# Adding the last six rounds' expert results into four sum rows per token, and reading the first ten rounds' rows early, in a fused attention and mixture-of-experts kernel

## The reference, cut to what matters

```
xe = jnp.zeros((E, CAP, H), x.dtype).at[sorted_e, pos].set(tok_sorted, mode='drop')
h = jax.nn.silu(jnp.einsum('ech,efh->ecf', xe, w1)) * jnp.einsum('ech,efh->ecf', xe, w3)
ye = jnp.einsum('ecf,ehf->ech', h, w2)
...
vals = jnp.where((pos < CAP)[:, None], vals, 0.0)
out = jax.ops.segment_sum(vals * flat_w[:, None], flat_t, num_segments=T)
shared = jax.nn.silu(x @ shared_gate.T) * (x @ shared_up.T) @ shared_down.T
return (out + shared).reshape(B, S, H)
...
x = x + _layernorm(_L0_ffn_ref(_layernorm(x, axis=-1), ...), axis=-1)
```

## Time and profile before

| what | us |
|---|---|
| median of three runs | 1123.37 |
| the profiled execution's own time | 1122.23 |
| its span, from first to last instruction | 1120.4 |
| first instruction of run_experts on TensorE | 948.8 |
| last DMA issue of run_experts on POOL ends | 1057.7 |
| first load of finish is issued | 1064.8 |
| last residual on VectorE ends | 1118.2 |

### The profile page before, as it was taken

How to read it: one execution, slowest core, us unless ns; L and a number is a source line. 1 busy time by engine, 2 the same in 40 slices (tenths; PEclk the granted TensorE clock), 3 DMA queues, 4 the chain that set the end, 5 groups by cost and what they waited for, 6 DMA issues and landing times. The chain is left out here.

```text
span 1120.4 us, 16485 instructions
## 1 busy us (share of the span) xinstructions
PE 911.1 (81%) x5190; PEld 289.5 (26%) x5190; DVE 816.9 (73%) x1314; ACT 685.9 (61%) x1416; POOL 555.9 (50%) x729
## 2 busy tenths in 40 slices
PE   5657999999999999999999999999986541745076
PEld 3311222222222222222222222222212321534043
DVE  6787888889889988988988998898841540322057
ACT  5714777777787777778778777777884210333113
POOL 6780020124356455645735554563576754456425
PEclk9867999999999999999999999999998665666578
DMA  5893432012332222222223212000222003410097
GB/s 140 262 250 63 118 80 62 15 38 47 83 110 87 90 90 55 59 49 82 82 91 104 49 39 50 5 6 14 79 82 91 2 3 90 119 51 13 17 400 275
DMA packets 107181, 96.35 MB, mean 86 GB/s; under 512 B 51406, under 2 KB 86512, under 8 KB 105046
## 3 DMA queue, kind: packets, MB, share of 16 engines
q1 hardware_dynamic: 89846, 88.12, 26.7%
q0 software_dynamic: 14336, 4.25, 1.8%
q10 hardware_dynamic: 2912, 2.93, 1.2%
HBM read 49.36 MB, written 65.24 MB: 102 GB/s over the span
## 5 line engine op out<-in xcount | busy, mean ns | idle before, releaser
L269 DVE TENSOR_REDUCE half_max<-s_pair 128x2 f32<-128x1024 f32 x512 | 602.0, 1218 | 77.8 <-PE s_pair L258 73.2
L1423 ACT ACTIVATE probs<-st_bank 128x512 f32<-128x512 f32 x1024 | 544.1, 602 | 170.3 <-PE st_bank L1519 157.2
L1285 POOL DMA_INDIRECT table<-rows,keys_i x256 | 255.5, 998 | 180.7 <-PE pv_bank L1528 67.5
L1519 PE MATMUL st_bank<-q_stack,k_stack 98*128 98x512 bf16 (+1 forms) x1024 | 324.0, 387 | 13.0 <-ACT probs L1423 4.9
L1528 PE MATMUL pv_bank<-probs,values 128*9 128x512 f32 x2048 | 267.7, 595 | 3.1 <-ACT unit_out L1358 2.8
L258 PE MATMUL s_pair<-k_stack,q_stack 64*128 64x512 bf16 x1024 | 202.5, 395 | 28.7 <-DVE half_max L269 26.4
L258 PEld LDWEIGHTS s_pair<-k_stack,q_stack 64*128 64x128 bf16 x1024 | 49.2, 93 | 344.3 <-issue 197.4
L1519 PEld LDWEIGHTS st_bank<-q_stack,k_stack 98*128 98x128 bf16 (+1 forms) x1024 | 77.7, 97 | 171.4 <-issue 86.2
L1721 POOL DMA_INDIRECT results<-out,ids x64 | 62.2, 971 | 53.7 <-ACT out L1783 37.3
L1754 DVE TENSOR_TENSOR h<-s_pair,gsig 128x256 f32<-128x256 f32 x16 | 6.8, 425 | 71.3 <-ACT gsig L1775 53.1
L1174 POOL CAST shift<-minus_max 128x16 bf16<-128x16 f32 x32 | 6.4, 201 | 101.2 <-DVE minus_max L275 101.1
(11 more groups left out here) (253 smaller groups left out, 845.9 us busy)
## 6 DMA issues: line engine op xcount, KB each, us to landing
results<-zeros SPq DMA_DIRECT2D x8, 2048.0 KB
choices<-results SPq DMA_DIRECT2D x6, 2048.0 KB, 23.7
table<-blank SPq DMA_DIRECT2D x8, 772.0 KB, 7.3
probs<-table SPq DMA_DIRECT2D x16, 386.0 KB
q_stack<-q_image SPq DMA_DIRECT2D x96, 64.0 KB
k_stack<-k_image SPq DMA_DIRECT2D x96, 64.0 KB
k_image<-k_piece SPq DMA_DIRECT2D x16, 256.0 KB, 3.3
table<-rows,keys_i POOLq DMA_INDIRECT x256
```

What stands on the lines that cost most here:

```text
L269: nc.vector.tensor_reduce(halves[:, h:HG:SIDE_HEADS, tile, half], stacks.s_pair[slot % S_SLOTS][:].rearrange("p (s k) -> p s k", s=SIDES), ...
L1285: pool.indirect_dma_start(out=table, out_offset=bass.IndirectOffsetOnAxis(ap=keys_i[c % 2][:, pick:pick + 1], axis=0), in_=rows[c % 2][:, ...
L1423: A.activation(probs[:, s % P_SLOTS, :], st_bank[at % ST_BANKS][:], ACT.Exp).then_inc(bank_free, 1)
L1519: M(bank(at)[:], k_stack[g][own, tile // PER, h, tile % PER * P:(tile % PER + 1) * P], q_stack[g][own, half, h, :], start=True, stop=True) ...
```

## The change

The last six of the 16 rounds (round 10, `ALONE`, and up) are no longer written into `results`. Their rows are added by the DMA itself (`compute_op=ALU.add`) into a new DRAM tensor `sums`, with 4 rows per token: expert q of each round adds into row token x 4 + q. Two adds into the same row must not be in flight together, so POOL waits, before the issue for expert q of round r, for the landing of the one for expert q of round r - 1. Unfilled slots have spare rows behind the real ones and are written too. `sums` is cleared beside `results` during attention, with 8 more DMAs of 1 MB.

Once the first ten rounds' puts have landed, SP loads all of `results` in 8 chunks of 2 MB into two buffers, `choices0` and the storage of `xfT`. For each chunk VectorE adds choices 0 to 5 (`sum_choices`), TensorE adds choices 6, 7 and `shared` (`part_products`), and VectorE writes the sum of both over `shared`. The first four chunks stand between rounds, the others behind the last round. `finish` then loads `sums`, 4 rows per token (8.4 MB), in the same 10 pieces; VectorE adds rows 0 and 1, TensorE rows 2, 3 and `shared`. DEEP goes from 7 to 5. POOL's own wait at the end is for the last round alone.

```diff
-Q, DEEP, OUT_DEEP = 4, 7, 5
+Q, DEEP, OUT_DEEP = 4, 5, 5
+ALONE = 10
+SUM_ROWS = N * Q
...
+                    width = PER * Q * DIM
+                    first = CLEAR_AT.index(n) * width
+                    sp.dma_start(sums[0:SUM_ROWS, :].rearrange("(p r) d -> p (r d)", p=P)[:, first:first + width].rearrange("p (o i) -> p o i", i=run),
+                                 zeros[:].rearrange("p (o i) -> p o i", o=1).to_broadcast([P, width // run, run])).then_inc(cleared, 16)
...
         @block.sync
         def _(sp):
 
             for r in range(DEEP, ROUNDS):
                 sp.wait_ge(turned, r - DEEP + 1)
-                sp.wait_ge(slot_read, 2 * (r - DEEP + 1))
+                sp.wait_ge(slot_read, SLOT_STEPS * (r - DEEP + 1))
                 rows_of.load_rows(sp, table, r)
+            all_alone(sp)
+            width = PER * TOPK * DIM
+            for c in range(CHUNKS):
+                if c >= 2:
+                    sp.wait_ge(part_steps, part_step(c - 2, PART))
+                sp.dma_start(choices[c % 2].rearrange("p t k d -> p (t k d)"),
+                             results.rearrange("(p r) d -> p (r d)", p=P)[:, c * width:(c + 1) * width]).then_inc(choices_in[c % 2], 16)
...
+                if r == ALONE:
+                    all_alone(pool)
...
+                    else:
+                        if r > ALONE:
+                            pool.wait_ge(put[q], put_before(q) + 16 * (r - ALONE))
+                        pool.indirect_dma_start(out=sums, out_offset=bass.IndirectOffsetOnAxis(ap=ids[a][:, q:q + 1], axis=0),
+                                                in_=out[a][:, q, :], in_offset=None, compute_op=ALU.add).then_inc(put[q], 16)
-            for r in range(ROUNDS - OUT_DEEP, ROUNDS):
-                put_of(pool, r)
+            put_of(pool, ROUNDS - 1)
...
+                else:
+                    V.tensor_scalar(ids[of][:, 0:1], xe[a][:, 0, ID:ROW], float(Q), None, ALU.mult)
+                    for q in range(1, Q):
+                        V.tensor_scalar(ids[of][:, q:q + 1], xe[a][:, q, ID:ROW], float(Q), float(q), ALU.mult, ALU.add).then_inc(slot_read, 1)
...
+            def sum_choices(c):
+
+                rows = choices[c % 2]
+                dve.wait_ge(choices_in[c % 2], 16 * (c // 2 + 1))
+                V.tensor_tensor(rows[:, :, 0:MINE // 2, :], rows[:, :, 0:MINE // 2, :], rows[:, :, MINE // 2:MINE, :], ALU.add).then_inc(part_steps, 1)
+                dve.wait_ge(part_steps, part_step(c, THREE))
+                V.tensor_tensor(rows[:, :, 0, :], rows[:, :, 0, :], rows[:, :, 1, :], ALU.add).then_inc(part_steps, 1)
+                dve.wait_ge(part_steps, part_step(c, PAIR_SUM))
+                V.tensor_tensor(rows[:, :, 0, :], rows[:, :, 0, :], rows[:, :, 2, :], ALU.add).then_inc(part_steps, 1)
+                dve.wait_ge(part_steps, part_step(c, ROW_SUM))
+                dve.wait_ge(part_ready, c + 1)
+                V.tensor_tensor(shared[:, c * PER:(c + 1) * PER, :], rows[:, :, 0, :], part_bank[c % 2][:].rearrange("p (t d) -> p t d", t=PER), ALU.add).then_inc(part_steps, 1)
...
+                if r >= ALONE + 2:
+                    sum_choices(r - ALONE - 2)
+            for c in range(ROUNDS - ALONE - 2, CHUNKS):
+                sum_choices(c)
...
+            def part_products(c):
+
+                if c >= 2:
+                    pe.wait_ge(part_steps, part_step(c - 2, PART))
+                to = part_bank[c % 2][:].rearrange("p (t d) -> p t d", t=PER)
+                M(to, ident[:], shared[:, c * PER:(c + 1) * PER, :], start=True, stop=False)
+                pe.wait_ge(choices_in[c % 2], 16 * (c // 2 + 1))
+                for k in range(MINE, TOPK):
+                    mm = M(to, ident[:], choices[c % 2][:, :, k, :], start=False, stop=(k == TOPK - 1))
+                mm.then_inc(part_ready, 1)
...
+                if r > ALONE:
+                    part_products(r - ALONE - 1)
+            for c in range(ROUNDS - ALONE - 1, CHUNKS):
+                part_products(c)
...
-        ADDED = TOPK // 2
+        ADDED = Q // 2
...
-            width = TOPK * DIM
+            width = Q * DIM
...
-                V.tensor_tensor(rows[c][:, :, 0:2, :], rows[c][:, :, 0:2, :], rows[c][:, :, 2:4, :], ALU.add).then_inc(summed, 1)
-                dve.wait_ge(summed, sum_step(c, PAIRS))
                 V.tensor_tensor(whole[:, tiles(c), :], rows[c][:, :, 0, :], rows[c][:, :, 1, :], ALU.add).then_inc(summed, 1)
```

More of the change, by code:

```diff
@@ L663, in ring_places, with attend_and_route @@
     return {user: place for place, user in enumerate(order)}
-def attend_and_route(nc, q_image, k_image, v_columns, bias_q_image, bias_k_image, consts, later, x_in, stacks, rows_of, w13, w2_t, table, results):
+def attend_and_route(nc, q_image, k_image, v_columns, bias_q_image, bias_k_image, consts, later, x_in, stacks, rows_of, w13, w2_t, table, results, sums):
     with ExitStack() as ctx:
@@ L1667, in _, with run_experts @@
             shared_down(7)
-def run_experts(nc, table, consts, rows_of, results):
+def run_experts(nc, table, consts, rows_of, results, sums):
     ROUNDS = E // Q
@@ L1845, in _, with finish @@
                     turn(r + 3)
-def finish(nc, consts, results, out):
+                if r > ALONE:
+                    part_products(r - ALONE - 1)
+            for c in range(ROUNDS - ALONE - 1, CHUNKS):
+                part_products(c)
+def finish(nc, consts, sums, out):
     with ExitStack() as ctx:
@@ L1861, in finish @@
         tiles = lambda c: pieces[c]
-        rows = [sb(f"choices{c}", [P, size(c), TOPK, DIM]) for c in range(len(pieces))]
+        rows = [sb(f"sums{c}", [P, size(c), Q, DIM]) for c in range(len(pieces))]
         whole = sb("whole", [P, TILES, DIM])
@@ L1899, in _ @@
                 pe.wait_ge(loaded[c], 16)
-                for r in range(ADDED, TOPK):
-                    mm = M(to, ident[:], rows[c][:, :, r, :], start=False, stop=(r == TOPK - 1))
+                for r in range(ADDED, Q):
+                    mm = M(to, ident[:], rows[c][:, :, r, :], start=False, stop=(r == Q - 1))
                 mm.then_inc(bank_done, 1)
@@ L1965, in program @@
     table = dram("table", [SLOT_ROWS, ROW])
-    results = dram("results", [RESULT_ROWS, DIM])
+    results, sums = dram("results", [RESULT_ROWS, DIM]), dram("sums", [SUM_ROWS + P * Q, DIM])
     row = lambda a, n: a.rearrange("(o d) -> o d", o=1).to_broadcast([P, n])
@@ L1989, in program @@
             rows_of = ExpertRows(held, nc, stacks)
-            attend_and_route(nc, q_image, k_image, v_columns, bias_q_image, bias_k_image, consts, later, x_in, stacks, rows_of, w13, w2_t, table, results)
-            run_experts(nc, table, consts, rows_of, results)
-        finish(nc, consts, results, out)
+            attend_and_route(nc, q_image, k_image, v_columns, bias_q_image, bias_k_image, consts, later, x_in, stacks, rows_of, w13, w2_t, table, results, sums)
+            run_experts(nc, table, consts, rows_of, results, sums)
+        finish(nc, consts, sums, out)
 def shape_constants():
```

69 lines of the change are left out of this document (44 added, 25 removed).

## The result

The changed kernel takes 1134.03 us (median of 5 runs, 1129.66 to 1134.78), the kernel before 1122.32 (5 runs): a ratio of 1.0091, 95% interval 1.0063 to 1.0119 (a ratio is taken over all runs and need not be the quotient of two medians). It is slower, by 10 to 12 us, where 10 us less were forecast, and it lies outside the range. The profiled execution took 1130.67 us with a span of 1128.7; before's were 1122.23 and 1120.4, so the traces differ by 8.3 us.

The account below looks back on a forecast made before the run. DMA engines were taken to idle while POOL paces the rounds, then everything waits for DMA. Run_experts 7.2 us longer and finish 17.5 shorter give 10.3 us off the 1123.4 median: 1113 us, range 1106 to 1130.

Parts of the forecast that it names:

- entry into run_experts: Start of run_experts: with five table loads ahead instead of seven, all engines enter earlier, a gain of 2.4 us.
- a chunk every: Early loads in run_experts: two buffers, each turning round in 11.3 us of load and sum, give a chunk every 5.65 us.
- finish lasts: Finish: half the bytes to load, VectorE sets the pace; 38.1 us against 55.6 before, a gain of 17.5 us.
- POOL's chain: Adding rounds: a round takes four issues, 5.1 us, or issue to landing if larger; 16 us of slack, lasting until about 7 us.
- the signs that the prediction gave for being wrong: In run_experts: POOL gaps before adds ended by DMA, rounds over 7 us, POOL releasing the meeting last, or long VectorE waits.
- the adding scatters become the bound: POOL's wait for the previous round's put: adds land slowly beside the stream, kernel slower, 1138 us at 12 us landing; chance 0.17.
- break-even, L = 9.6 us: Adding rounds: the landing time of an adding scatter, 9.6 us, at which the changed kernel would be as long as before.
- Landing takes 7.5 us: Scatters in run_experts: a landing takes 7.5 us instead of 2.2, loads start 5.3 us later, time 1118 us; chance 0.20.
- Late reading: Run_experts: SP's put wait or VectorE's place holds chunk 2 until the rounds end; 8 us more, 1121 us; chance 0.03.
- The page's rule: Scatters beside the bulk load: DMA engines alternate between queues by whole packets, so landing is 3 to 4 us, changing no term.
- clears at nothing: During attention: eight extra 1 MB clears cost nothing, as DMA is busy 29% there; uncovered, each would be 2.4 us.
- side sum for 358 GB/s: Chunk loads: at the skill's 358 GB/s chunks would come every 6.1 us and finish 3.5 us later; 429 GB/s was used.

Follow-up runs that it names:

- run 1: Changed kernel with all loads of results and chunk sums behind the last round's adding scatters, so the adds run without the stream: 1162.61 us, ratio 1.0376.
- run 5: Changed kernel with ALONE = 12, so twelve rounds written plainly and four added: 1132.83 us, ratio 1.0109.
- run 8: Changed kernel with chunks 2 to 7 loading only half their bytes, result incomplete: 1124.07 us, ratio 1.0032.
- run 2: Changed kernel with plain scatters into sums in place of adds, waits and stream kept, result incomplete: 1118.18 us, ratio 0.9991.
- run 6: Kernel before with DEEP = 5 and a tiny POOL memset behind POOL's last waits as a mark: 1119.82 us, ratio 1.0001.
- run 9: Kernel before with SyncE instead of POOL waiting at the block's end for the last five rounds' result scatters: 1120.57 us, ratio 0.9981.
- run 7: Changed kernel with each 2 MB chunk loaded in four DMAs with 4 KB rows instead of one with 16 KB rows: 1123.21 us, ratio 1.0029.
- run 3: Changed kernel with a bounds check on the adds that drops the rows of empty slots: 1128.46 us, ratio 1.0088.
- run 11: Changed kernel with VectorE's first add of each chunk cut from 128x1536 to 128x4, output incomplete: 1133.16 us, ratio 1.0103.

## Why the prediction was wrong

Against its own steps (the times are of the profiled execution):

| step | forecast | measured |
|---|---|---|
| entry into run_experts | 2.4 us less | 1.4 less |
| plain scatter, start to landing | 2.2 | 2.5 |
| chunk 0 issued | 1020.3 | 1021.46 |
| a chunk every | 5.65 | 6.16 |
| last sum ends | 1070.4 | 1075.8 |
| adding round on POOL | 5.1 | 10.1 |
| finish starts | 1072 | 1088.9 |
| finish lasts | 38.1 | 39.8 |

The last two rows are the whole miss: 16.9 + 1.7 = 18.6 us between 1110.1 and 1128.7.

**The step that failed is "POOL's chain": "At 2.2 us nothing waits: POOL is done about 1054 and has 16 us of slack."** It gave an adding scatter the issue time and the landing of a plain one on idle queues, and the stream beside it only 1.1 us, charged to the chunks. Three things stood in its place. (1) The instruction costs POOL 1.84 us with its gap instead of 1.27 (run 1): 7.4 us a round. (2) Beside the stream an adding scatter is seen to land after 8.5 to 11.1 us instead of 3.3 (run 1), mostly just behind a chunk (runs 5 and 8); a plain one lands after 7 to 8.5 us (run 2). Stream without addition leaves a round at 7.5 us, addition without stream at 7.4, and both together give 10.1. (3) POOL's way out of the block, 5.5 us behind its last landing (runs 6 and 9), was in no term. Finish therefore starts 9.9 us after POOL's last row does, 4.4 for the landing and 5.5 for the exit. Before, the same stretch took 8.0 us, which the prediction read as a bound for the landing. Of the signs that the prediction gave for being wrong, gaps ended by DMA, a round of over 7 us and POOL as the last to release the meeting all came.

**The rivals.** The right one was "the adding scatters become the bound", given 0.17. Its place (POOL's wait for round r - 1) holds, and so in the main does its reason, that each row of an add takes a turn of its own beside the stream (rows below). Its break-even, L = 9.6 us, was too high, since it lacked the exit. To end where before ended, finish would have to start at 1120.4 - 39.8 = 1080.6; from the first add at 1022.3, with 6.3 us between the first and last row of a round and the 9.9 us behind it, that leaves (1080.6 - 1022.3 - 6.3 - 9.9) / 5 = 8.4 us a round, an estimate from this trace. By the rival's formula finish would start at 1020.3 + 6 x 10.1 + 3.8 + 0.5 = 1085.2; measured 1088.9. "Landing takes 7.5 us" was wrong on idle queues: the quiet it leaned on is POOL's exit. Beside the stream it happens to be near the plain scatters' 7 to 8.5 us, and run 2, which comes nearest to this case, gives a ratio of 0.9991 where 1118 against 1123.4 was priced. "Late reading" did not happen.

**The page's rule, and the rows of the queues.** The prediction cited the Trainium skill, "DMA: Bandwidth & Descriptors", section "Queues, rings and completion order", for a scatter waiting behind one or two rows of 16 KB, 3 to 4 us. The section counts a packet as some 9 to 17 descriptors, where the profile's "packets" are single rows. A chunk gives each of 16 engines 128/16 = 8 rows: by that count a whole chunk's share, by estimate 2.1 MB at 429 GB/s = 4.9 us, may pass in one turn. The trace does not bear that out for the rows that it records. It shows the scatters (q0) and the chunk loads (q1) side by side; from 1028 to 1033 us, and from 1033.5 to 1034.5, when chunk 1 has hardly a row left (records, MB, and the records' summed times as a share of 16 engines):

```profile
q1 hardware_dynamic: 140, 2.06, 100.8%
q0 software_dynamic: 140, 0.06, 10.1%
```

```profile
q0 software_dynamic: 366, 0.17, 138.9%
q1 hardware_dynamic: 15, 0.05, 21.8%
```

In number the rows pass one for one while the chunk is read (60 and 61 from 1062.5 to 1065 us, 113 and 122 in 4.5 us of run 5), and the rest of the adds go at once behind it. So it is the data that come late, not only the sign that they have landed. What the prediction missed is the number of turns: an adding scatter has 143 records, some 9 on each engine, a plain one 29. At 0.6 us for a row of 16 KB that is, by estimate, 5.4 us for each adding scatter in the queue. Rows of 4 KB (run 7) let the adds through more than twice as fast, 229 records in 3 us:

```profile
q1 hardware_dynamic: 250, 0.93, 81.8%
q0 software_dynamic: 229, 0.11, 28.8%
```

The section also says that a DMA's semaphore is written only after every earlier write of that DMA engine, over all queues. Whether that adds to the landings here, no run shows.

**What was right.** Finish within 1.7 us, with the loads gone from its bound; the chunks' place within 1.2 us and their pace within 0.5 (the last sum, 5.4 us late, still hidden behind POOL); clears at nothing that shows, since SP's first table load comes no later than before (940.97 against 943.06). Entry was over by 1.0 us. The side sum for 358 GB/s is off, which nothing hangs on: by the prediction's own steps chunk 7 would land 4.8 us later, not finish start 3.5.

**Open.** Why an adding scatter holds POOL 0.57 us longer (run 3 excludes the bytes of the spare rows), and why beside the stream its first record comes more than 4.5 us after POOL's row starts (1022.33, none until 1026.90), where on idle queues it comes within 2.3 (1025.19 to 1027.5 in run 1).

## What to carry to other kernels

When a chain of dependent scatters is moved beside a bulk load, price its landing at the time of the load in flight, not at the idle landing; here 3.3 us became 8.5 to 11.1 for adds, and 2.5 became 7 to 8.5 for plain scatters. Large loads beside such a chain should be cut into DMAs with shorter rows, which took back two thirds of the loss here, and before DMA idle time is filled it should be asked which chain made it idle: that chain pays. Let an engine that is slow to leave a block not be the one that waits at its end.

## What was not expected of the hardware

- An adding indirect scatter shows about one DMA record for each of its rows, 143 in all, a plain one 29. Beside the stream, the 24 scatters of run 2 (plain) and of the changed kernel, in windows of 46 and 60 us (packets, MB, share of 16 engines):

```profile
q0 software_dynamic: 706, 1.45, 8.3%
```

```profile
q0 software_dynamic: 3431, 1.56, 23.5%
```

  For nearly the same bytes, five times the packets and 14.1 us of all 16 engines instead of 3.8. The chunks still came every 6.2 us, against 6.4 with plain ones.
- POOL's indirect rows grow beside VectorE's addition of two SBUF tensors, plain from 0.95 to as much as 2.47 us (run 2), adding from 1.54 to 2.3 (the changed kernel; run 11 shows VectorE as the cause). The Trainium skill, "SBUF — State Buffer", section "Who interferes with whom", says that a VectorE instruction with two SBUF inputs contends with a GpSimd instruction that reads SBUF; run 11 agrees, taking the scatter's reading of its indices as such a read, which no run tests.
- POOL takes 5.5 us to leave a block in which it has issued scatters, behind a wait for their landing (5.53 us, run 6) or without one (5.53 us, run 9). No run shows whether a block without scatters costs it less.
